# One decoder layer on one core: the rows that enter cross-attention stored as columns and added into the slots, and the end of the first stage cut down

## What is computed

```
x = layernorm(x + attn(x));  x = layernorm(x + xattn(x, ctx));  x = layernorm(x + ffn(x))
```

## Time and profile before

| | us |
|---|---|
| median of 3 runs | 1306.13 |
| the profiled execution | 1305.99 |
| its span | 1304.3 |
| PE busy | 1178.8 (90%) |
| DVE busy | 903.4 (69%) |
| ACT busy | 708.9 (54%) |
| POOL busy | 252.2 (19%) |
| mean granted TensorE clock | 0.946 of full |

### The profile page before, as it was taken

One profiled execution on the slowest core, in us unless ns is written; L12 is line 12 of the kernel. 1 busy time (PEld: TensorE's weight loads), 2 busy tenths in 40 slices (PEclk: granted clock), 3 DMA queues, 4 the chain that ended last, 5 costly groups with the idle time before them and its releaser, 6 DMA issues. The chain is left out here.

```text
span 1304.3 us, 19625 instructions
## 1 busy us (share of the span) xinstructions
PE 1178.8 (90%) x6282; PEld 990.1 (76%) x6282; DVE 903.4 (69%) x2060; ACT 708.9 (54%) x1244; POOL 252.2 (19%) x277
## 2 busy tenths in 40 slices
PE   4889899799999999999999999999734999999991
PEld 3557678578877787887788787788634999999991
DVE  5654645677774668777466877746784888888884
ACT  3435446356673336667333666732313767767772
POOL 2110110000000000000000000000022777777761
PEclk8898997799999999999999999999956999999996
DMA  8201001000001010000100000063183223222224
GB/s 272 77 1 49 17 1 33 25 1 1 1 1 33 9 17 1 1 1 1 33 9 17 1 1 1 1 236 121 65 288 93 42 42 47 40 44 44 42 35 141
DMA packets 49945, 61.42 MB, mean 47 GB/s; under 512 B 9297, under 2 KB 41491, under 8 KB 49747
## 3 DMA queue, kind: packets, MB, share of 16 engines
q1 hardware_dynamic: 40292, 48.44, 11.4%
q0 software_dynamic: 8832, 12.11, 5.9%
q10 hardware_dynamic: 754, 0.03, 0.0%
HBM read 46.07 MB, written 14.50 MB: 46 GB/s over the span
## 5 line engine op out<-in xcount | busy, mean ns | idle before, releaser
L77 PE MATMUL x_psum<-x_s_lo,x_kq_hi 128*128 128x512 f32 (+1 forms) x312 | 126.2, 405 | 4.5 <-DVE x_mx L1308 3.7
L1113 POOL TENSOR_TENSOR x_sq<-x_sq 128x512 f32<-128x512 f32 x12 | 15.5, 1294 | 568.1 <-ACT x_sq L1099 568.1
L77 PE MATMUL x_psum<-x_p_lo,x_v_hi 128*128 128x512 f32 (+1 forms) x312 | 124.4, 399 | 0.0
L78 PE MATMUL x_psum<-x_s_hi,x_kq_lo 128*128 128x512 f32 (+1 forms) x312 | 123.6, 396 | 0.0
L79 PE MATMUL x_psum<-x_s_hi,x_kq_hi 128*128 128x512 f32 (+1 forms) x312 | 123.5, 396 | 0.0
L79 PE MATMUL x_psum<-x_p_hi,x_v_hi 128*128 128x512 f32 (+1 forms) x312 | 123.3, 395 | 0.0
L78 PE MATMUL x_psum<-x_p_hi,x_v_lo 128*128 128x512 f32 (+1 forms) x312 | 123.3, 395 | 0.0
L1308 DVE CUSTOM_DVE_ANT_0 x_e<-x_psum,x_rsb,x_rs 128x512 f32<-128x512 f32 (+1 forms) x117 | 86.4, 747 | 49.5 <-PE x_psum L79 48.5
L77 PE MATMUL e_bank<-e_w_lo,e_g_hi 128*128 128x256 f32 x368 | 107.7, 293 | 0.1
L77 PE MATMUL e_bank<-e_xT_lo,e_w_hi 128*128 128x256 f32 x368 | 105.1, 286 | 2.1 <-DVE e_xT_lo L2002 1.4
L78 PE MATMUL e_bank<-e_xT_hi,e_w_lo 128*128 128x256 f32 x368 | 104.8, 285 | 0.0
(11 more groups left out here) (365 smaller groups left out, 3203.3 us busy)
## 6 DMA issues: line engine op xcount, KB each, us to landing
w<-in_w SPq DMA_DIRECT2D x16, 1024.0 KB, 11.9
x_rsb<-scratch_thin_inv SPq DMA_DIRECT2D x12, 256.0 KB, 3.9
x_rsb<-scratch_thin_rs SPq DMA_DIRECT2D x9, 256.0 KB, 4.0
h_x<-in_x SPq DMA_DIRECT2D x4, 512.0 KB, 6.0
sT<-in_xT SPq DMA_DIRECT2D x4, 512.0 KB, 7.2
h_w<-in_mlp_w SPq DMA_DIRECT2D x2, 1024.0 KB, 10.2
scratch_x<-h_x SPq DMA_DIRECT2D x4, 512.0 KB, 2.9
x_x<-scratch_x SPq DMA_DIRECT2D x4, 512.0 KB, 8.5
```

The costliest lines, as they stand in the source:

```text
L77: pe.matmul(out, w_hi, x_lo, start=start, stop=False)
L78: pe.matmul(out, w_lo, x_hi, start=False, stop=False)
L1113: pool.tensor_tensor(sq[:, 0], sq[:, 0], sq[:, 1], ALU.add).then_inc(sum_ok, 1)
```

## The change

**Columns in place of rows.** The head no longer stores x1 as rows but the columns `sT` (`store_x1`, into a DRAM tensor `x1T`), so its store waits for the turned columns and no longer for the rows; the block's end no longer waits for the stores. In the third iteration DVE adds the columns to the finished slots, one more operation per (c, h), before PE turns them. So the turned rows are already x1 + slots: `add_rows` becomes `moments`, which reads the banks; `apply` reads the banks too, and PE's next `turn_rows` waits for `apply` of the chunk before instead of for the adds. The router's product of x1 alone (`raw_logits`, `take_logits`) goes; its column sums (`sums_mm`) stay, in a place near the head's end. `turn_rows` works half by half.

**The GRU's order.** In the third iteration `moments(c)` and `logits(c)` now stand closer: `logits(2)` in (3, 0) where it stood in (3, 1), `logits(1)` in (2, 1) where it stood in (3, 0). `apply` stands in (2, 0), (2, 1) and (3, 0), behind z, and `apply(LAST)` at the block's end instead of in the next block.

**The head.** Squares of context rows move from chunks 1 to 3 to chunks 0 to 2, the roots of the context from chunk 3's step 3 to chunk 2's, the value work is spread over steps of chunks 2 and 3, the third chunk's `square_sums` and `rms` move from the end to chunk 3's step 6. Six of the eight slot splits move behind the block's end into the first iteration.

**Route.** The last chunk's rows are stored ahead of the expert loads; the gates are stored from ACT's queue.

```diff
     def store_x1(c):
-        sp.wait_ge(x1_ok, (c + 1) * TPC)
-        sp.dma_start(rows_of(io["x1"])[:, c * TPC:(c + 1) * TPC], x[:, c % 3]).then_inc(x1_out, 16)
+        sp.wait_ge(x1_sb, DH * (c + 1))
+        sp.dma_start(io["x1T"].rearrange("(c p) t -> p c t", p=P)[:, :, chunk(c)], sT[:, :, chunk(c)]).then_inc(first["x1_out"], 16)
...
+    VALUES32_AT = {(2, 5): 1, (2, 7): 2, (LAST, 1): 0, (LAST, 3): 3}
+    VALUES_HI_AT = {(2, 6): 1, (LAST, 0): 2, (LAST, 2): 0, (LAST, 4): 3}
+    VALUES_LO_AT = {(LAST, 0): 1, (LAST, 2): 2, (LAST, 4): 0, (LAST, 5): 3}
...
+                    if c == LAST and f == 6:
+                        pe.wait_ge(hT_lo_ok, DH * NC)
+                        first["square_sums"](pe, 0, c - 1, 2)
...
+            pe.wait_ge(first["ld_rout"], 48)
+            for h in range(DH):
+                last = pe.matmul(bank[7][:, 0:NE], ones[:], first["rout_w"][:, h], start=(h == 0), stop=(h == DH - 1))
+            last.then_inc(sums_mm, 1)
             turn_x1(LAST)
-            raw_logits(LAST - 1)
-            raw_logits(LAST)
...
                         v.tensor_tensor(s, s, new, ALU.add).then_inc(s_ok, 1)
+                        if not more:
+                            v.wait_ge(s_ok, i + 1)
+                            v.wait_ge(x1_back[c], 16)
+                            v.tensor_tensor(s, s, x1_cols[c][:, h], ALU.add).then_inc(added, 1)
...
                 def turn_rows(c):
-                    pe.wait_ge(s_ok, it * GH + (c + 1) * DH)
                     pe.wait_ge(mult_ok, (it + 1) * NC)
                     if c >= 1:
-                        pe.wait_ge(added, c * DH)
+                        pe.wait_ge(x2_ok, c * TPC)
+                    for h in range(DH):
+                        pe.wait_ge(added, c * DH + h + 1)
...
             act.activation(pr[:], lg[:], ACT.Exp).then_inc(exp_ok, 1)
-            for j in range(TPC):
-                t = NT - TPC + j
-                act.activation(x2[:, j], x2[:, j], ACT.Identity, bias=nb[:, t:t + 1], scale=rs[:, t:t + 1]).then_inc(x2_ok, 1)
+            act.wait_ge(gates_ok, TOP)
+            act.dma_start(io["x2"].rearrange("(t p) d -> p t d", p=P)[:, :, D:], gate_rows[:]).then_inc(kept, 16)
```

More of the change, by code:

```diff
@@ L839, in turn_x1 @@
                     pe.wait_ge(hT_lo_ok, DH * NC)
+                    pe.wait_ge(first["rs_ok"], LAST)
                 else:
@@ L947, in _ @@
                     piece(i)
-                    if c == LAST and i == BORDER[c][0] + 1:
-                        pe.wait_ge(z_ok, DH * NC)
-                        first["square_sums"](pe, 0, c - 1)
                 if c >= 1 and a < NC:
@@ L1257, in _ @@
                             slots_hi(act, it + 1, c, 0)
-            apply(2)
+            apply(LAST)
         @block.vector
@@ L1262, in _, with moments @@
             k = Chain(v, vchain, steps0)
-            def add_rows(c):
-                v.wait_ge(x1_back[c], 16)
-                for i in range(DH):
-                    v.wait_ge(turn_mm, c * DH + i + 1)
-                    v.tensor_tensor(x2_rows[c][:, 2 * i:2 * i + 2], bank[6 + i].rearrange("p (t d) -> p t d", d=D),
-                                    x2_rows[c][:, 2 * i:2 * i + 2], ALU.add).then_inc(added, 1)
-                v.wait_ge(added, DH * (c + 1))
+            def moments(c):
+                v.wait_ge(turn_mm, c + 1)
                 for j in range(TPC):
-                    k.mark(v.bn_stats(c_stats[:, j], x2_rows[c][:, j]))
+                    k.mark(v.bn_stats(c_stats[:, j], bank[6 + j // 2][:, j % 2 * D:(j % 2 + 1) * D]))
                 v.wait_ge(vchain, k.base + k.n)
@@ L1353, in updates_lo @@
                     v.tensor_tensor(u_part(p_lo, c), u32[c % 2][:], u_part(p_hi, c).bitcast(F32), ALU.subtract).then_inc(u_lo_ok, 1)
+                if it == 0:
+                    for c in range(1, LAST):
+                        for h in range(DH):
+                            slots_lo(v, it, c, h)
+                    slots_lo(v, it, LAST, 0)
                 slots_lo(v, it, LAST, DH - 1)
@@ L1441, in _ @@
                             normed(c + 2)
-                        if not more and (c, h) in ((2, 0), (3, 0), (3, 1)):
-                            logits(c + h - 2)
                         if not more and (c, h) in ((1, 1), (2, 1), (3, 0)):
-                            add_rows(c - 1)
+                            moments(c - 1)
+                        if not more and (c, h) in ((2, 0), (2, 1), (3, 0)):
+                            logits(c + h - 2 if c < LAST else 2)
                         v.wait_ge(n_ok, i + 1)
+                        if i == 0:
+                            v.wait_ge(x1_out, 16 * NC)
                         k.step(v.tensor_tensor(s, s, new, ALU.subtract))
```

177 lines of the change are left out of this document (74 added, 103 removed).

## The result

The changed kernel takes 1292.37 us (median of 4 runs, 1289.17 to 1295.76), the kernel before 1306.41 beside it. The ratio is 0.9899 with a 95% interval of 0.9865 to 0.9932. Timed again later, it took 1290.8 us (6 runs), a ratio of 0.9885 (0.9865 to 0.9906); one of the 11 executions of the kernel before that stood beside it was a slow one of 2338.87 us and is left out of the ratio. The forecast was 1292.8.

What follows compares the result with a forecast made beforehand. PE was taken as nearly full except at three joints, the first two set by DVE and the third by the gates' store behind weights. Head -5.7, tail -4.2 and joint -3.3 took 1305.99 to 1292.8 us; range 1286.5 to 1299.

Steps and rivals of the forecast that it cites:

- Head's end: End of the head, up to the first score: DVE's shorter queue brings the first score from 254.43 to 244.6, -9.8 us.
- The splits behind the joint: First iteration, ahead of the first scores: six moved slot splits cost 0, bounds 0 and +3.7 us.
- values32(2): Head, chunk 2's step 7: DVE's values multiplication stands before the norm chain, +1.1 us, bounds 0 and +2.4.
- Square sums: Head, step 6 of chunk 3: PE's square sums, moved from a wait at the end, cost +1.3 us, bounds 0 and +1.9.
- each step of DVE stays under PE: 0: Head, chunk 3: lighter ACT, DVE's steps near 2.5 us under PE's 2.85, so no change.
- Clock of chunk 2: Head, start of chunk 2: after longer PE idling it may begin at 1.2 GHz, +1.7 us, bounds 0 and +3.5.
- Tail: Last GRU steps of the third iteration: shorter DVE queue, block ends near 948.4 instead of 952.6, -4.2 us, bounds -6 and 0.
- Joint: Route to the experts' start: gates no longer stored behind the weights, first expert product earlier, -3.3 us, bounds 0 and -6.
- all 1.7 us of casts in place of 0.4: Experts' start: by the skill's rule POOL's casts would be added whole, the sum ending at 1293.8; the forecast took 0.4.
- the store waits behind the weights after all: Rival at route's end: gates' store still waits though on another queue, joint +2.3 instead of -3.3, 1298.4 us; chance 0.1.
- the ring: Rival in the GRU's tail: PE's turns, ACT's apply and DVE's logits wait in a circle, tail +12.3, 1309.3 us; chance 0.03.
- the head gives little: Rival in the head: clock, held values32(2) and splits cancel the -9.8 to 0, 1298.5 us; chance 0.15.

## Why the prediction was right, step by step

The total is 0.6 us off, but the terms miss by up to 1.7 with both signs; that the sum came so near is luck in part.

- *Head's end, -9.8*: right (-9.27), and DVE's part was right to 0.2 us. But not DVE ends it now: ACT's square does, 1.7 us later than forecast, behind PE's slower pieces and turning. The splits (4.0) and raw logits (3.1), each put back alone, lengthen it; the rest wasn't tried. The splits behind the joint, forecast at 0, cost next to nothing: PE waits for one 0.65 us, and the stretch to the first `arg` is 0.4 us shorter than before in the profile whose first scores began at half the clock as before, and 1.05 where they ran at the full clock.
- *values32(2), +1.1*: right (+1.13).
- *Square sums, +1.3*: their cost was sized too low, 2.2 us and above its bound of 1.9, since it left out the roots on DVE; and "each step of DVE stays under PE: 0" left out a wait of 0.56 us that stood in the earlier trace rows. The two errors cancelled, and the clock's rise did the rest: +1.12 in all.
- *Clock of chunk 2, +1.7 as half of 3.5*: the profile shows +1.6, but as a chance, not a half: it is 1.6 in four profiles and 0 in six (49.3 less 1.13 is the 48.2 of before). So meeting 1.7 is luck. And the kernel before has it too: beside 48.23 us stands 49.03 in the run with the stores moved, whose clock read 0.50 in that joint. With two profiles before, how much of the term is the change's is open, and that longer idle time is its cause isn't shown.
- *Tail, -4.2*: -2.5 in the first profile. Where the clock doesn't fall it is 532.3 - 536.5 = -4.2, but not by the sum: the stretch that the sum covers gave 3.2 to 3.7, because DVE, taken as running without a gap, waits 2.6 us in it for ACT and PE (first profile); 0.8 came from the two steps ahead, one of them with `logits(1)`, which the sum took as free beside PE's gates; that step is 1.55 longer. The fall of the clock was not foreseen. No run undid a part of the tail alone, so what its moves are worth is read from these rows, not tried.
- *Joint, -3.3*: -3.9, by two errors of opposite sign. The weights landed 32.1 us behind route's start (34.6 in my sum), so that ACT began its splits 2.3 us sooner than forecast (33.0, not 35.3), and from there to the product it took 5.8 us where I had 4.1: DVE's splits lost 1.9 us to POOL's casts where I allowed 0.4. The sum's last terms, as they stand (986.4 + 0.7 + 1.6 + 0.6), give 989.3 and not 987.9; and all 1.7 us of casts in place of 0.4 would have given 1294.1, not 1293.8. The rule that I had set against my rows, of the Trainium skill (GPSIMD Engine Reference, 1. Specifications), says that GpSimd contends with DVE instructions that have two SBUF inputs. It gives no size; adding the whole 1.7 us, as I did for it, comes within 0.2 us of what DVE lost.
- *Rivals*: "the store waits behind the weights after all" fell, since the gates had landed at 963.3; the ring fell (0.30 us of waiting ahead of the turn that it was to hold); "the head gives little" fell.

## What to carry to other kernels

Before an operation is moved out of a joint, look at what else would stand in its place: the square sums filled a wait that was still there after they had gone, and cost 2.2 us where they went. A store that the next stage needs shouldn't be issued behind bulk loads on one queue; and a load that is long done should have its own semaphore, so that nobody waits for its neighbours. Where two engines hold each other, moving the operation of one by a step may only change who waits, as the values' multiplication did; holding the casts, which nobody needed yet, gave DVE its time back. And look where the clock rises before two stretches are compared: two of the sizes above changed by 0.5 to 1 us when it was taken into account.
